# Attention stage by pairs of tiles, and the self term of the second layer as a matmul with diagonals

## The reference

```
h = relu(layernorm(x))                                   # before each layer
# layer 0: diffusion plus attention
deg = clip(adj.sum(1), 1);  dis = deg ** -0.5
diffusion = (dis[:,None] * adj * dis[None,:]) @ h - h
sim  = h @ h.T / (norm[:,None] * norm[None,:])
attn = softmax(beta * sim * adj, axis=1)
x = x + diffusion + sigmoid(alpha) * (attn @ h - h)
# layer 1: self term beta1[i] * h[i]
x = x + (1 / (adj.sum(1) + beta1))[:,None] * (adj @ h + beta1[:,None] * h) @ kernel + bias
# layer 2 and layer 3 follow: adj_hat @ (h @ W), and a hyperbolic layer
```

## Time and profile before

| | us |
|---|---|
| median of three runs | 1001.25 |
| lowest, highest of them | 991.61, 1002.87 |
| the profiled execution | 997.35 |
| its span in the trace | 995.5 |
| busy in it: PE, DVE, ACT, POOL | 881.7, 645.5, 511.8, 322.2 |
| first product of the attention, start of its last tail | 61.42, 478.37 |

### The profile page before, as it was taken

How to read it: one execution, slowest core, us unless ns; L and a number is a source line. 1 busy time by engine, 2 the same in 40 slices (tenths; PEclk the granted TensorE clock), 3 DMA queues, 4 the chain that set the end, 5 groups by cost and what they waited for, 6 DMA issues and landing times.

```text
span 995.5 us, 19959 instructions
## 1 busy us (share of the span) xinstructions
PE 881.7 (89%) x6528; PEld 513.1 (52%) x6528; DVE 645.5 (65%) x1902; ACT 511.8 (51%) x1124; POOL 322.2 (32%) x380
## 2 busy tenths in 40 slices
PE   0188989889898989888999999999999999999992
PEld 0155656556565656555455554454445555545551
DVE  5987988798889888888334432333214766754666
ACT  4878786778777778655311220111105466535334
POOL 3664454545445454443211121000002222212221
PEclk9999999999999999999999999999999999999997
DMA  7979595859595958200000000000000000000100
GB/s 222 278 224 247 173 261 156 231 154 263 152 253 148 248 171 240 65 1 2 1 1 1 1 1 1 1 1 1 1 1 1 1 1 1 1 1 1 43 22 22
DMA packets 84787, 89.36 MB, mean 90 GB/s; under 512 B 71296, under 2 KB 76544, under 8 KB 76544
## 3 DMA queue, kind: packets, MB, share of 16 engines
q1 hardware_dynamic: 81088, 88.09, 31.0%
q10 hardware_dynamic: 3648, 0.61, 0.3%
HBM read 69.81 MB, written 2.10 MB: 72 GB/s over the span
## 4 chain that ended last, share of the span: by engine, by line
PE 45%; issue 20%; DVE 17%; POOL 12%; DVEq 3%; ACT 1%; DMA 1%; ACTq 0%; POOLq 0%; SPq 0%
PE ps_acc L1212 26%; POOL e_parts L333 10%; PE ps_acc L1154 7%; PE ps_s L1140 5%; PE ps_t L1212 3%; DVE e_parts L763 3%; DVE ps_s L757 2%; POOL hyp L361 2%; PE ps_s L1280 1%; DVE ez L687 1%; PE ps_s L1243 1%; PE ps_t L1268 1%; DMA x<-in_x 1%; PE ps_s L1277 1%; ACT e_parts L557 1%
## 5 line engine op out<-in xcount | busy, mean ns | idle before, releaser
L333 POOL CAST e_parts<-ez 128x512 f16<-128x512 f32 x256 | 190.4, 746 | 213.4 <-ACT ez L484 203.4
L1154 PE MATMUL ps_acc<-h_a,e_parts 128*128 128x129 f16 x3072 | 223.3, 222 | 38.4 <-DVE e_parts L763 23.0
L1154 PEld LDWEIGHTS ps_acc<-h_a,e_parts 128*128 128x128 f16 x3072 | 191.8, 98 | 124.6 <-DVE e_parts L763 61.9
L484 ACT ACTIVATE ez<-ps_s,scal 128x512 f32<-128x512 f32 x256 | 191.4, 771 | 68.5 <-DVE ps_s L757 68.4
L763 DVE TENSOR_TENSOR e_parts<-ez,e_parts 128x512 f16<-128x512 f32 x256 | 189.0, 739 | 46.3 <-POOL e_parts L333 46.3
L1140 PE MATMUL ps_s<-u_t 128*128 (+1 forms) x768 | 211.3, 385 | 7.2 <-ACT ez L484 6.8
L1212 PE MATMUL ps_acc<-adj_t,stage 128*128 128x512 fp8e4 x896 | 199.9, 379 | 0.0
L757 DVE TENSOR_TENSOR ps_s<-ps_s,adj_t 128x512 f32<-128x512 f32 x256 | 176.6, 690 | 9.7 <-PE ps_s L1140 7.7
L1212 PE MATMUL ps_acc<-adj_t,h_a 128*128 128x512 fp8e4 x768 | 169.3, 379 | 0.0
L438 ACT ACTIVATE bytes<-stage 128x1024 uint8<-128x1024 f32 x128 | 134.3, 1049 | 35.8 <-DMA stage<-in_adj 35.8
L1212 PEld LDWEIGHTS ps_acc<-adj_t,stage 128*128 128x128 f16 x896 | 86.8, 98 | 97.6
(11 more groups left out here) (159 smaller groups left out, 752.5 us busy)
## 6 DMA issues: line engine op xcount, KB each, us to landing
stage<-in_adj SPq DMA_DIRECT2D x64, 1024.0 KB, 5.5
x<-in_x SPq DMA_DIRECT2D x4, 512.0 KB, 9.9
out<-x SPq DMA_DIRECT2D x8, 256.0 KB, 2.2
adj_t<-bytes SPq DMA_TRANSPOSE x64, 3.2
kernel_sb<-in_L_gnn_kernel ACTq DMA_DIRECT2D x1, 64.0 KB, 6.6
w_sb<-in_L_gnn_W ACTq DMA_DIRECT2D x1, 64.0 KB, 7.4
embed_top<-in_L_gnn_embed ACTq DMA_DIRECT2D x1, 64.0 KB, 7.9
embed_top<-in_L_gnn_layer ACTq DMA_DIRECT2D x1, 64.0 KB, 6.7
```

The costliest lines, as they stand in the source:

```text
L333: g.tensor_copy(e_parts[:, HI, s % RING, :], ez[:, s % RING, :]).then_inc(ehi_done, 1)
L484: a.activation(ez[:, s % RING, :], ps_s[:, s % RING, :], ACT.Exp, scale=beta_s, bias=shift_c).then_inc(exp_done, 1)
L1154: last = t.matmul(att_acc[:, b, 0:D + 1], e_parts[:, re, s % RING, P * b:P * (b + 1)], h_a[:, s, rh, 0:D + 1], start=(s == 0 and n == 0 an ...
```

## The change

**Pairs.** Two neighbouring tiles are one unit of 1024 columns for DVE, ACT and POOL: `z_pair`, `exp_pair`, `high_pair` and `low_pair`, 128 of each. PE's matmuls stay as they are, but a semaphore is now given for each pair. The scores go to three pairs of banks (`score_banks`), of which the third is `ps_t`. `ez` and `e_parts` keep their size and hold two pairs. DVE's mask product runs one pair ahead of the subtraction, PE's scores three pairs ahead of its products.

**Chunk end.** `att_evac` copies the accumulators to SBUF (`att_sb`) and frees them; the division and the sum into x (`att_tail`) come two subtractions later and read the copy.

**Casts.** One quarter of adj follows each exp of a pair, twelve quarters ahead (`CAST_AHEAD`). Six instead of eight halves are cast ahead of the attention. The first pair of a chunk waits for the chunk's first four halves, the ninth pair for the other four. The hd steps stand at pairs 7 to 15 of the last chunk.

**Code.** The stage is written out: its loops are gone, and so is the register arithmetic in them.

**Layer 1.** Its self term is added on PE within the aggregation, as a product with diagonal matrices of twice beta (high and low f16 parts in `diag`, twelve matmuls of 128 columns for a chunk). ACT writes the high part (`diag_high`) and DVE the low part in layer 0. `turn_h` and `prepare` leave layer 0, with ACT's copy and DVE's update.

The diff, cut to its core:

```diff
-Z_AHEAD = 2
-EARLY = 2
-CAST_AT = [3 * m + r for m in range(HPC) for r in (1, 2)]
-HD_AT = [8 + 6 * m for m in range(4)]
+PAIRS = NP * NCH
+BANKS = 3
+CAST_AHEAD = 12
+SUM_AT = [7, 9, 11, 13]
+HD_AT = [8, 10, 12, 14]
+LOW_AT = [9, 11, 13, 15]
...
-T_AFTER = ([w + 6 for w in W_0], (), [20, 25, 36, 41, 52, 57, 68, 73], ())
+T_AFTER = ((), (), [20, 25, 36, 41, 52, 57, 68, 73], ())
...
+        diag = u_t[:, :, :].rearrange("p r (k f) -> p r k f", f=D)
...
+        score_banks = (ps_s[:, 0:2, :], ps_s[:, 2:4, :], ps_t[:, :, :])
...
-            def high_part(s, base):
-                pool.wait_ge(exp_done, base + s + RING + 1)
-                pool.wait_ge(e_used, base + s + 1)
-                g.tensor_copy(e_parts[:, HI, s % RING, :], ez[:, s % RING, :]
+            def high_pair(p):
+                pool.wait_ge(exp_done, p + 1)
+                if p >= 2:
+                    pool.wait_ge(e_used, 2 * p - 2)
+                at = 2 * p % RING
+                g.tensor_copy(e_parts[:, HI, at:at + 2, :], ez[:, at:at + 2, :]
...
-            def exp_step(s, base):
-                act.wait_ge(z_done, base + s + 1)
-                act.wait_ge(elo_done, base + s + 1)
-                a.activation(ez[:, s % RING, :], ps_s[:, s % RING, :], ACT.Exp, scale=beta_s,
+            def exp_pair(p):
+                act.wait_ge(z_done, p + 1)
...
+                if p >= 2:
+                    act.wait_ge(elo_done, p - 1)
+                at = 2 * p % RING
+                a.activation(ez[:, at:at + 2, :], score_banks[p % BANKS], ACT.Exp, scale=beta_s,
...
+            for p in range(PAIRS):
+                exp_pair(p)
+                if p + CAST_AHEAD < PAIRS:
+                    cast_quarter(p + CAST_AHEAD)
+                if p // NP == NCH - 1 and p % NP in HD_AT:
+                    high_hd(HD_AT.index(p % NP))
...
+            def diag_high(m):
+                for b in range(BC):
+                    k = ds(BC * m + b, 1)
+                    last = a.activation(diag[:, HI, k, :].rearrange("p a f -> p (a f)"), ident32,
+                                        ACT.Copy, scale=beta2[:, k])
+                last.then_inc(diag_hi, 1)
...
+            def z_pair(p):
+                c, k = p // NP, p % NP
+                if k % (NP // 2) == 0:
+                    for at in adj_turned:
+                        dve.wait_ge(at, 16 * (BC * c + BC // 2 * (1 + k // (NP // 2))))
+                dve.wait_ge(s_done, p + 1)
+                pair = score_banks[p % BANKS]
+                v.tensor_tensor(pair, pair, adj_u8[:, k, CW * c:CW * (c + 1), :]
+                                .rearrange("p i t -> p t i"), ALU.mult).then_inc(z_done, 1)
+            def low_pair(p):
+                dve.wait_ge(ehi_done, p + 1)
+                at = 2 * p % RING
+                v.tensor_tensor(e_parts[:, LO, at:at + 2, :], ez[:, at:at + 2, :],
+                                e_parts[:, HI, at:at + 2, :], ALU.subtract).then_inc(elo_done, 1)
+            def att_evac(c):
+                dve.wait_ge(e_used, NB * (c + 1))
+                v.tensor_copy(att_sb[:, :, :], att_acc[:, :, 0:D + 1]).then_inc(acc_free, 1)
+                dve.drain()
...
+            z_pair(0)
+            for p in range(PAIRS):
+                c, k = p // NP, p % NP
+                if p + 1 < PAIRS:
+                    z_pair(p + 1)
+                if c and k == 0:
+                    att_evac(c - 1)
+                low_pair(p)
+                if c and k == 1:
+                    att_tail(c - 1)
+                if c < NCH - 1 and k == 3:
+                    x_minus_h(slice(2 * c, 2 * c + 2), slice(BC * c, BC * (c + 1)))
+                if k == (5 if c == NCH - 1 else 8):
+                    degrees(c)
+                if c == NCH - 1:
+                    if k == SUM_AT[0]:
+                        for at in adj_turned:
+                            dve.wait_ge(at, 16 * BC * NCH)
+                    if k in LOW_AT:
+                        low_hd(LOW_AT.index(k))
+                        dve.drain()
+                    if k in SUM_AT:
+                        sum_hd(SUM_AT.index(k))
...
-                dve.wait_ge(prep_done, m + 1)
-                dve.wait_ge(bias_in, m + 1)
-                update_x(inv_beta, prep_out, m)
+                dve.wait_ge(diag_hi, m + 1)
+                for b in range(BC):
+                    k = ds(BC * m + b, 1)
+                    last = v.scalar_tensor_tensor(diag[:, LO, k, :].rearrange("p a f -> p (a f)"),
+                                                  ident32, beta2[:, k],
+                                                  diag[:, HI, k, :].rearrange("p a f -> p (a f)"),
+                                                  ALU.mult, ALU.subtract)
+                last.then_inc(diag_ok, 1)
...
-            def scores(s, base, col):
-                pe.wait_ge(exp_done, base + s + 1)
-                k = s % NB
+            def scores(g_s):
+                p, c, k = g_s // 2, g_s // NB, g_s % NB
+                if g_s % 2 == 0 and p >= BANKS:
+                    pe.wait_ge(exp_done, p - BANKS + 1)
                 for n, (rj, ri) in enumerate(((HI, HI), (HI, LO), (LO, HI))):
-                    last = t.matmul(ps_s[:, s % RING, :], u_t[:, rj, P * k:P * (k + 1)],
-                                    u_t[:, ri, col], start=(n == 0), stop=(n == 2))
-                last.then_inc(s_done, 1)
-            def att_products(s, base, i):
-                if s % BC == 0:
+                    last = t.matmul(score_banks[p % BANKS][:, g_s % 2, :],
+                                    u_t[:, rj, P * k:P * (k + 1)],
+                                    u_t[:, ri, CW * c:CW * (c + 1)], start=(n == 0), stop=(n == 2))
+                if g_s % 2:
+                    last.then_inc(s_done, 1)
...
+                if c and s == 0:
+                    pe.wait_ge(acc_free, c)
+                if s % 2 == 0:
+                    pe.wait_ge(elo_done, g_s // 2 + 1)
...
+            for p in range(NP * (NCH - 1)):
+                scores(2 * (p + BANKS))
+                scores(2 * (p + BANKS) + 1)
+                att_products(2 * p)
+                att_products(2 * p + 1)
...
+                if L == 1 and q == NB // BC - 1:
+                    pe.wait_ge(diag_ok, c + 1)
+                    for b in range(BC):
+                        for rh, rd in ((HI, HI), (HI, LO), (LO, HI)):
+                            t.matmul(acc[:, P * b:P * (b + 1)], h[:, BC * c + b, rh, :],
+                                     diag[:, rd, BC * c + b, :], start=False, stop=False,
+                                     skip_group_check=True)
```

More of the change, by code:

```diff
@@ L230, in _ @@
         def _(sp):
[L232 to L235 removed]
+            for s in (w_done, l_split):
+                sp.sem_inc(s, 1)
             for n in range(NG):
@@ L821, in _ @@
-            for s in range(EARLY, NB):
-                if s + Z_AHEAD < NB:
-                    z_step(s + Z_AHEAD, NB * (NCH - 1), slice(CW * (NCH - 1), N), NCH - 1)
-                low_part(s, NB * (NCH - 1))
-                if s == EARLY:
-                    degrees(NCH - 1)
-                if s + 1 in HD_AT:
-                    sum_hd(HD_AT.index(s + 1))
-                if s - 3 in HD_AT:
-                    low_hd(HD_AT.index(s - 3))
+            x_minus_h(slice(NP - 2, NP), slice(NB - BC, NB))
@@ L845, in _ @@
             v.reciprocal(inv_deg, inv_deg)
-            dve.drain()
-            v.tensor_tensor(inv_beta, inv_deg, l1b, ALU.mult)
             dve.drain()
```

203 lines of the change are left out of this document (76 added, 127 removed).

## The result

| | before | after |
|---|---|---|
| median, us | 999.82 | 949.29 |
| lowest, highest (four runs of each) | 991.61, 1002.87 | 947.61, 949.92 |
| ratio of the times, 95% interval | | 0.9504 (0.9445 to 0.9564) |
| span of the profiled execution | 995.5 | 945.8 |

A forecast was written before the change was run, and what follows sets the result against it. PE was taken to bound the kernel, at 2.68 us a pair. Span 995.5 - 41.9 (attention stage) - 5.4 (layers 0 and 1) = 948.2, 950.1 with the 1.85 around it; forecast 951 us, range 930 to 980.

The forecast's parts named there:

- PE bounds a pair at 2.68 us: Attention chunks: PE needs 2.68 us a pair, the chain of dependences 2.4, so PE is last with 0.3 in hand.
- A chunk of 46.0: Attention chunk: 42.9 us of PE's own pace, 2.5 for the chunk's end and 0.6 for late loads.
- the tail's: After a chunk's end: the tail takes DVE 1.8 us, slack takes up 0.7, so 1.1 reach PE.
- The 0.6 for the loads' lateness: Loads of adj in each attention chunk: just hidden behind PE; 0.6 us a chunk allowed, bounds 0 and 3.
- I count the low clock as gone: Chunk ends: PE's idle of 0.7 us, a third of the earlier one, no longer brings the clock's drop; 6.8 us before.
- The first score stays at 56.34: Start of the attention stage: first score unchanged at 56.34 us, first products at 63.5, 2.1 later than before.
- 6.9 for two pairs: Last chunk: an hd step's loop takes 6.9 us against PE's 5.36, three times 1.5 more; the chunk 52.7.
- Layers 0 and 1: Layers 0 and 1: PE's turn and product give way to twelve f16 matmuls a chunk; 5.4 us less, bounds 10.7 and 0.
- rival 1: Chunk ends and hd loops: the rings absorb nearly all, a chunk is 42.9 + 0.7 us, the whole 930; chance 0.13.
- Rival 2: Each pair: POOL's cast and DVE's subtraction clash, the chain is 2.95 us, a chunk 49, the whole 972; chance 0.18.
- rival 3: Attention pairs: PE's short waits keep the clock at 0.50; a third of the pairs gives 1065 us, slower; chance 0.03.
- rival 4: Attention chunks: copy and pairs only shift the wait, a chunk keeps its 50 us, the whole about 990; chance 0.04.

The follow-up runs named there:

- experiment 3: The changed kernel without the copy of the accumulators; the tail reads them in PSUM, ahead of the new chunk's first subtraction: 945.05 us, ratio 0.9467.
- experiment 1: The kernel before with only layer 1's self term as a matmul with diagonals, nothing of the attention stage changed: 991.64 us, ratio 0.9921.
- experiment 4: The changed kernel with a chunk's sixteen casts of adj packed behind its first twelve exps: 991.68 us, ratio 0.9937.

## Why the prediction was right, point by point

- **PE bounds a pair at 2.68 us**: 2.67 in mid-chunk, with PE alone in the chain. Exp 1.199 (1.20 taken), DVE's two 1.222 and 1.226 (1.24), POOL's cast 1.121 (1.10), of which the median is 1.041: the mean holds 16 of 128 casts that waited for DVE.
- **A chunk of 46.0**: 45.75 to 46.32. Its parts were less good than their sum. The copy's wait was put at 0.7 and is 0.90; the tail's at 1.1 and is 1.57, because the scaling instruction waits out a cast (1.08; the shortest of the eight has 0.23), which no row of before had shown (the same instruction, L771, takes 0.23 to 0.51 there); `x_minus_h` and degrees were put at 0.7, and in the second chunk PE has no wait behind them. The 0.6 for the loads' lateness is nearly nothing: halved loads gain 1 us at most in the whole.
- **"I count the low clock as gone"**: right, but its argument, the length of the wait, is only half shown. In the attention stages of all fourteen traces the drop came only behind single waits of 1.97 us and more at a chunk's end. But among those the length does not decide. In the kernel before the wait is 1.97 or 1.98 at six ends; the low clock followed at three of them, and at the other three it did not, as at this one, beside the earlier trace rows:

```profile
216.87 1.03 PE L1154 MATMUL ps_acc<-h_a,e_parts 128*128 128x129 f16 x12 [1.97 <-DVE x L775]
217.74 0.81 PE L1140 MATMUL ps_s<-u_t 128*128 x3
```

  In experiment 3 it followed waits of 2.38 and 2.43 and not another of 2.38. What decides is not shown. Nor does the low clock alone make "the difference between chunks of 50 and of 53": PE is busy 1.8 us longer there (46.79 for 44.97), and with halved loads the chunks with and without it are 47.9 to 48.1 and 46.8 to 46.9. So most of the 3 us goes with late loads.
- **Start: "The first score stays at 56.34"** was wrong. It came at 53.57, and the first products at 61.01 for 63.5. The first vector instruction runs at 5.65 us for 8.96, waiting for x's first load. Of the eleven profiles of kernels with the new stage two had it at 7.4 to 7.6 and the others at 5.5 to 5.7, and the first score followed: 56.08 and 55.72 in those two. The three with the old stage have 8.95 to 9.00. So the 2.8 us come from ahead of the attention, and the start also varies among kernels that do not differ there. What sets them was not tried.
- **Last chunk: "6.9 for two pairs"** was mis-sized: 7.75. The loop was put together from the durations alone; the cast that `low_hd` waits out adds 0.84 us, which is the size of the difference. The last chunk took 56.72 for 52.7; three loops that are 0.85 us longer explain 2.6 of these 4.0, the rest was not traced. With the first chunk's 41.86 for 44.2 and the start's 2.5 the misses of 4.0 and 4.8 cancel, so that the stage's end at 435.32 lies so near to the 436.4 foretold is luck.
- **Layers 0 and 1**: put at 5.4 us. From the stage's end to the span's end the trace after has 6.7 us less (510.5 for 517.1), and experiment 1 gives 6.3 as a difference of medians.
- **Rivals.** The rings do not absorb the tail (rival 1). Rival 2 had a real mechanism, the clash between POOL and DVE, but mostly at the ends, beside `x_minus_h` and in the hd steps, not in each pair. Rivals 3 and 4 fell with the clock and the chunks. Their chances are not carried over rightly: rival 3 (0.03) is the slower one and rival 4 (0.04) the one near no change, while the prediction gives slower 0.04 and within 1% 0.03.

Where the gain comes from cannot be added up from single undos: without the wide instructions 17 us are lost, with the casts bunched 42, and the layers gave 6 on the kernel before, which is more than 50. Width and spread casts overlap, because a late load holds the exps. The prediction named the casts as a cause of waits before, but not their weight: some 25 us of before's time are late loads, half of the whole gain.

## What to carry to other kernels

Where a load is used by an instruction that stands in the same queue as the critical work, first ask how evenly those instructions lie over the load's period. Halving the load tells within one run whether it matters, if one also looks at how long the half takes and what waits are left. When such a change has made one engine the bound, count the next one's busy time in the same window: at 90% of it, the one attempt here to move its work about gave nothing, and taking a copy of 0.70 us off it gave 2.6 us (by moving it to ACT) and 4.2 (by leaving it out). It is otherwise in a loop that crosses engines, as in the last chunk: there one producer, put one step earlier than its consumer needed it, gave 5 us.

## What was not expected of the hardware

- A POOL cast of 1024 f32 columns from SBUF and several kinds of DVE instruction with SBUF operands do not run together: the later one waits until the other ends, down to instructions of four columns: the scaling L776 took 230 to 1081 ns, median 1079, in the kernel after, and the division of the degrees, which multiplies by a constant and has one input, 169 to 876 ns. Two of the casts took 2.12 us for 1.04. The mask product, with an operand in PSUM, was never held and held no cast: its longest of 128 is 1233 ns, and of the 80 casts that begin while one runs the longest is 1.04 us. The trace, over the eight of each (count, shortest, median, longest in ns):

```profile
L776 DVE TENSOR_SCALAR small<-small,scal x8: 230/1079/1081, 107.3 to 436.4; 128x4 f32<-128x4 f32 x8
```
```profile
L791 DVE TENSOR_SCALAR cols<-cols x8: 169/170/876, 81.2 to 395.1; 128x4 f32<-128x4 f32 x8
```

  The Trainium skill, "SBUF — State Buffer", the section on who interferes with whom, says that the pair of ports that DVE shares with POOL is locked for a whole instruction, for DVE instructions with two SBUF inputs and for copies, casts and `tensor_scalar` in a mode with two ports, but never for `tensor_reduce`. The rows agree. In the kernel after no reduction (L788) begins while a cast runs, but in the kernel of experiment 4 six do, and keep their 0.16 us, while the division behind them waits out the same cast:

```profile
138.88 1.07 POOL L332 CAST e_parts<-ez 128x1024 f16<-128x1024 f32 x1 [1.09 <-ACT ez L480]
138.96 0.16 DVE L791 TENSOR_REDUCE cols<-deg_parts 128x4 f32<-128x16 f32 x1
...
139.20 0.77 DVE L794 TENSOR_SCALAR cols<-cols 128x4 f32<-128x4 f32 x1
```
- Equal idle times of PE at a chunk's end, 1.97 us in the kernel before and 2.38 in that of experiment 3, were followed by matmuls at a lower clock at some ends and not at others. One of 2.10 was not, and 0.90 and 1.57 with two pairs between them were not either.
